# Two attention stages of one kernel: the order of scores, transposes, values and outputs on TensorE, and the last unit's end

## What is computed

```
# third block, the attention in front of the experts (x: 16 x 64 x 256, 16 heads of 16)
h = layernorm(x)
q, k, v = (h@wq+bq)*16**-0.5, h@wk+bk, h@wv+bv     # by head
p = softmax(q @ k.T)                                # 64 x 64 for each batch and head
x = x + (p @ v) @ wo + bo                           # then the experts

# fifth block, latent attention with a rotary part, causal
Q = concat(Qc, rope(Qr)); K = concat(Kc, rope(Kr))  # 16 + 8 wide
scores = where(causal, clip(Q @ K.T, -80, 80), -inf)
x = x + (softmax(scores / sqrt(24)) @ V) @ W_O
```

## Time and profile before

| | |
|---|---|
| time, median of 3 runs | 900.33 us (899.58 to 900.87) |
| the profiled execution: its own time, its span | 903.07 us, 901.3 us |
| PE, PEld busy, instructions | 763.8 us (85%), 510.4 us (57%), 7000 each |
| DVE, ACT, POOL busy | 569.3 us (63%), 428.8 us (48%), 314.9 us (35%) |
| granted TensorE clock over the span | 0.922 |
| block stage, first scores to last add | 440.04 to 481.73 |
| latent stage, first scores to last add | 789.33 to 830.95 |

### The profile page before, as it was taken

The page is one execution under the profiler, slowest core; times in us unless marked ns, Lnnn a source line. Parts: engine busy times, 40 slices in busy tenths (PEclk is TensorE's granted clock), DMA queues, the critical chain, the costliest instruction groups (busy, mean ns, idle before and its releaser), DMA issues. The chain is left out here.

```text
span 901.3 us, 19146 instructions
## 1 busy us (share of the span) xinstructions
PE 763.8 (85%) x7000; PEld 510.4 (57%) x7000; DVE 569.3 (63%) x1295; ACT 428.8 (48%) x1281; POOL 314.9 (35%) x379
## 2 busy tenths in 40 slices
PE   5999999698799999967777299999388886777996
PEld 4788888445333333345456288888267774365334
DVE  3565555539699999976796533222578776455474
ACT  3656666462565664234365100000367883655572
POOL 2111120027577888721350440100554432233002
PEclk9899999897799999998897599999679997989899
DMA  8011530000020000000001046542456310000001
GB/s 260 18 43 53 191 108 1 2 1 1 24 71 0 1 1 1 0 1 1 1 2 48 24 132 195 181 135 76 140 164 218 105 42 1 1 3 3 0 1 49
DMA packets 44893, 51.79 MB, mean 57 GB/s; under 512 B 7072, under 2 KB 40832, under 8 KB 44544
## 3 DMA queue, kind: packets, MB, share of 16 engines
q1 hardware_dynamic: 40256, 43.48, 15.5%
q0 software_dynamic: 1536, 4.20, 1.6%
q10 hardware_dynamic: 3008, 2.88, 0.9%
HBM read 45.31 MB, written 5.24 MB: 56 GB/s over the span
## 5 line engine op out<-in xcount | busy, mean ns | idle before, releaser
L968 PE MATMUL r_u_ps<-r_t_in,l_same_head 128*128 128x512 f32 x124 | 69.5, 643 | 1.4 <-DVE r_t_in L892 0.2
L1362 ACT ACTIVATE a_prob<-a_s_ps,a_negmax 128x256 f32<-128x256 f32 x128 | 59.1, 485 | 19.5 <-DVE a_negmax L1418 19.5
L936 POOL TENSOR_TENSOR r_q_in<-r_state,rec_q 128x512 f32<-128x512 f32 x62 | 68.0, 1097 | 0.0
L1737 ACT ACTIVATE a_prob<-a_s_ps,a_negmax 128x256 f32<-128x256 f32 x128 | 58.6, 482 | 19.4 <-DVE a_negmax L1773 18.4
L2334 PE MATMUL m_h_ps<-m_rowsT,l_w 128*128 128x256 f32 x256 | 58.7, 390 | 0.0
L1424 DVE COPY a_probT<-a_w_ps 128x512 f32<-128x512 f32 x48 | 31.5, 688 | 38.9 <-PE a_w_ps L1283 38.9
L1773 DVE TENSOR_REDUCE a_negmax<-a_s_ps 128x2 f32<-128x512 f32 x64 | 41.2, 684 | 22.6 <-PE a_s_ps L1653 19.7
L2334 PEld LDWEIGHTS m_h_ps<-m_rowsT,l_w 128*128 128x128 f32 x256 | 50.3, 197 | 7.2
L2345 PE MATMUL m_y_ps<-l_w,m_hidden 128*128 128x256 f32 x240 | 53.9, 379 | 0.0
L2380 ACT ACTIVATE m_rowsT<-m_xt_ps,l_B_s,l_B_g 128x256 f32<-128x256 f32 x16 | 8.2, 560 | 93.3 <-PE m_xt_ps L2322 86.7
L2248 DVE TENSOR_SCALAR m_hidden<-m_h_ps,l_b 128x256 f32<-128x256 f32 x64 | 28.0, 480 | 37.9 <-PE m_h_ps L2334 37.9
(11 more groups left out here) (388 smaller groups left out, 1881.5 us busy)
## 6 DMA issues: line engine op xcount, KB each, us to landing
l_w<-in_B_w SPq DMA_DIRECT2D x16, 1024.0 KB, 5.8
a_ctxT<-in_ctxT SPq DMA_DIRECT2D x31, 256.0 KB, 2.8
a_ctx<-in_ctx SPq DMA_DIRECT2D x16, 256.0 KB, 2.8
expert_out<-m_y ACTq DMA_DIRECT2D x7, 256.0 KB, 5.7
all_X<-in_x SPq DMA_DIRECT2D x4, 256.0 KB, 5.2
l_b<-in_B_b SPq DMA_DIRECT2D x1, 1024.0 KB, 5.3
all_xnT<-own_rows SPq DMA_DIRECT2D x1, 1024.0 KB, 6.5
routed_rows<-ffn_xn SPq DMA_DIRECT2D x8, 128.0 KB, 1.8
```

What stands on the lines that cost most here:

```text
L936: ins = nc.gpsimd.tensor_tensor(q_in[i % 2][m][:, :, :, :], twice(state[i % 2][m]), steps("q", 2 * i - 1, 2, m), ALU.mult)
L968: nc.tensor.matmul(u_ps[m][:, :, :, :], same_head[:, :], t_in[m][:, :, :, :], start=False, stop=True).then_inc(u_mm[m], 1)
L1362: ins = nc.scalar.activation(prob[n % 2][:, r, m, :], s_ps[r][:, m, :], ACT.Exp, bias=negmax[n % 2][:, r, m:m + 1], accum_out=den[n % 2][: ...
L1737: ins = nc.scalar.activation(prob[n % 2][:, r, m, :], s_ps[r][:, m, :], ACT.Exp, bias=negmax[n % 2][:, r, m:m + 1], accum_out=den[n % 2][: ...
```

## The change

- TensorE: scores(0) and scores(1) come first; then, in unit u, scores(u+2) stands behind the transposes of u and ahead of output(u-1) and values(u). In the last unit output(2) stands ahead of the transposes instead of behind them.
- The last unit's end is cut in two halves, one for each row tile: values, take_heads, output and add each run by half. The second half's values go into `s_ps0` and its output into `s_ps1`, which are free by then.
- The last unit's fourth scaling runs on VectorE instead of GpSimd, behind add(1).
- Latent stage alone (`bounded`): ScalarE takes one take_transposed(u) and one exps(u+1) in turn, and VectorE runs each sum with its reciprocal behind it, instead of each sum one ahead.

```diff
-                    pe.wait_ge(p_ready, ONE + 4 * u + n + 1)
+                    pe.wait_ge(*((last_p, ONE + 1) if (u, n) == (NU - 1, 3) else (p_ready, ONE + 4 * u + n + 1)))
...
+                    if u == NU - 1:
+                        pe.wait_ge(shifted_ready, ONE + 4 * NU)
                     of = {where(q): q for q in range(16)}
                     for i in range(2):
+                        out = last_o[i] if u == NU - 1 else o_ps[:, i, :, :]
...
-                    mm.then_inc(pv_mm, 1)
+                        if i == 1 or u == NU - 1:
+                            mm.then_inc(pv_mm, 1)
...
                 scores(0)
+                scores(1)
                 for u in range(NU):
-                    if u + 1 < NU:
-                        scores(u + 1)
+                    if u == NU - 1:
+                        output(u - 1)
                     for n in range(4):
                         transposes(u, n)
-                    if u >= 1:
+                    if u + 2 < NU:
+                        scores(u + 2)
+                    if 1 <= u < NU - 1:
                         output(u - 1)
                     values(u)
-                output(NU - 1)
+                for i in range(2):
+                    last_output(i)
...
+                def last_output(i):
+                    pe.wait_ge(heads_ready, ONE + NU + i)
+                    pe.wait_ge(x_added, ONE + NU - 1)
+                    for k in range(KD):
+                        mm = nc.tensor.matmul(last_out[i], headsT[:, i, k, :], WoT[:, k, :], start=(k == 0), stop=(k == KD - 1))
+                    mm.then_inc(out_mm, 1)
...
                 for u in range(NU):
-                    for r in range(4):
+                    for r in range(3 if u == NU - 1 else 4):
                         pool.wait_ge(rden_ready, ONE + 4 * u + r + 1)
...
+                def take_last_heads(i):
+                    act.wait_ge(pv_mm, ONE + NU + i)
+                    act.wait_ge(out_mm, ONE + NU - 1)
+                    if bv is None:
+                        ins = nc.scalar.activation(headsT[:, i, :, :], last_o[i], ACT.Copy)
+                    else:
+                        for m in range(KD):
+                            ins = nc.scalar.activation(headsT[:, i, m, :], last_o[i][:, m, :], ACT.Identity, bias=bv[:, m:m + 1])
+                    ins.then_inc(heads_ready, 1)
...
                 for u in range(NU):
-                    for r in range(3):
+                    for r in range(4):
+                        if not bounded and r == 3 and u + 1 < NU:
+                            exps(u + 1, 0)
                         take_transposed(u, r)
-                    if u + 1 < NU:
-                        exps(u + 1, 0)
-                    take_transposed(u, 3)
-                    if u + 1 < NU:
+                        if bounded and u + 1 < NU:
+                            exps(u + 1, r)
+                    if not bounded and u + 1 < NU:
                         for r in range(1, 4):
                             exps(u + 1, r)
...
-                    sums(u, 0)
+                    if not bounded:
+                        sums(u, 0)
                     for r in range(4):
-                        if r + 1 < 4:
+                        if bounded:
+                            sums(u, r)
+                        elif r + 1 < 4:
                             sums(u, r + 1)
                         reciprocals(u, r)
                     if u >= 2:
                         add(u - 2)
+                dve.wait_ge(rden_ready, ONE + 4 * NU)
+                nc.vector.tensor_tensor(of_bank(NU - 1, 3), of_bank(NU - 1, 3), rden[(NU - 1) % 2][:, 3, :].unsqueeze(2).to_broadcast([P, 8, T]), ALU.mult).then_inc(last_p, 1)
                 add(NU - 2)
-                add(NU - 1)
+                for i in range(2):
+                    dve.wait_ge(out_mm, ONE + NU + i)
+                    if bo is not None:
+                        dve.wait_ge(bias_added, ONE + NT)
+                    nc.vector.tensor_tensor(X[:, NT - 2 + i, :], last_out[i], X[:, NT - 2 + i, :], ALU.add).then_inc(x_added, 1)
```

More of the change, by code:

```diff
@@ L1914, in batch_attention_stage @@
         out_ps = sc.ps("out_ps", [P, 2, D])
-        (s_mm, top_ready, shifted_ready, exp_done, den_ready, rden_ready, p_ready, pt_mm, pt_ready, pv_mm, heads_ready, out_mm, x_added, bias_added) = (sc.sem(n) for n in (
-            "s_mm", "top_ready", "shifted_ready", "exp_done", "den_ready", "rden_ready", "p_ready", "pt_mm", "pt_ready", "pv_mm", "heads_ready", "out_mm", "x_added", "bias_added"))
+        (s_mm, top_ready, shifted_ready, exp_done, den_ready, rden_ready, p_ready, pt_mm, pt_ready, pv_mm, heads_ready, out_mm, x_added, bias_added, last_p) = (sc.sem(n) for n in (
+            "s_mm", "top_ready", "shifted_ready", "exp_done", "den_ready", "rden_ready", "p_ready", "pt_mm", "pt_ready", "pv_mm", "heads_ready", "out_mm", "x_added", "bias_added", "last_p"))
+        last_o = [o_ps[:, 0, :, :], s_ps[0][:, :, :].rearrange("p h t -> p (h t)")[:, 0:KD * P].rearrange("p (m q) -> p m q", m=KD)]
+        last_out = [out_ps[:, 0, :], s_ps[1][:, :, :].rearrange("p h t -> p (h t)")[:, 0:D]]
         def of_bank(u, r):
@@ L1968, in values @@
                                     pair = 4 * m + r
-                                    mm = nc.tensor.matmul(o_ps[32 * r:32 * r + 32, i, m, j * T:(j + 1) * T], vblk[:, 4 * u + 2 * i + j, pair, :],
+                                    mm = nc.tensor.matmul(out[32 * r:32 * r + 32, m, j * T:(j + 1) * T], vblk[:, 4 * u + 2 * i + j, pair, :],
                                                           probT[u % 2][:, of[i, pair], j * T:(j + 1) * T], start=True, stop=True)
-                    mm.then_inc(pv_mm, 1)
+                        if i == 1 or u == NU - 1:
+                            mm.then_inc(pv_mm, 1)
                 def output(u):
@@ L2030, in _ @@
                 for u in range(NU):
-                    for r in range(3):
+                    for r in range(4):
+                        if not bounded and r == 3 and u + 1 < NU:
+                            exps(u + 1, 0)
                         take_transposed(u, r)
-                    if u + 1 < NU:
-                        exps(u + 1, 0)
-                    take_transposed(u, 3)
-                    if u + 1 < NU:
+                        if bounded and u + 1 < NU:
+                            exps(u + 1, r)
+                    if not bounded and u + 1 < NU:
                         for r in range(1, 4):
                             exps(u + 1, r)
-                    take_heads(u)
+                    if u + 1 < NU:
+                        take_heads(u)
+                for i in range(2):
+                    take_last_heads(i)
             @block.vector
```

## The result

The changed kernel is slower: 903.79 us (median of 20 runs, 899.61 to 906.23) against 901.07 (20 runs, 899.58 to 903.61). The ratio is 1.0021, 95% interval 1.0011 to 1.0031, so +1.9 us where 1.15 less was forecast; the forecast had the sign wrong, and the median is outside its range. (Its sum was laid on 900.33, the median of three runs; on the 901.07 of twenty it would have been 899.9, which changes nothing of this.) The profiled execution has a span of 903.0 us (901.3 before) and a mean clock of 0.919 (0.922).

The account below looks back on a forecast made before the run. VectorE bounds the block stage; in the latent stage no engine is full and the loop round the engines sets the pace. Block +0.3 and latent -1.45 give -1.15 on 900.33: 899.2 us, range 897.3 to 901.1.

Parts of the forecast that it names:

- a stall of 0.5 on the full engine: Block stage loop: scores(3) waits for shift(2), output(0) comes later, and VectorE waits 0.5 us for add(0).
- 1.15 lost: Block stage end: output(2) ahead of the last transposes makes values(3) start at 478.1 against 476.95, 1.15 us later.
- The halves: Block stage end cut in halves: 3.9 us from values(3)'s start to the end against 4.78, a gain of 0.88.
- The sum of +0.3: Block stage in total: 1.15 us lost before values(3) less 0.88 gained by the halves, +0.3.
- The sum was -1.45: Latent stage in total: values(3) starts 0.45 us earlier and the end by halves gains 1.0, -1.45.
- I expect the stop again: Latent stage: TensorE's stop for late instructions comes again within values(0)'s last instructions, 1.2 to 1.5 us.
- It is given back at once: Latent stage loop: scores(3) starts 3.4 us earlier, but output(0) and values(1) now follow it, leaving 0.55 at transposes(2).
- The end by halves: Latent stage end: 3.54 us from values(3)'s start to the last add's end against 4.54, a gain of 1.0.
- number 2: Rival: the latent stage's instruction stop does not come back; -2.6 us, 897.7 us; chance 0.27.
- number 3: Rival: clock falls in the block stage while TensorE idles 2.75 us before output(2); about +2.0, 902.4 us; chance 0.10.
- Number 4: Rival: halved end and early scores give more than counted, no give-back in the latent stage; -3; chance 0.03.
- signs of being wrong: Last transposes not held by output(2), block-stage clock below 1.0 behind 470, or another stage moved by a microsecond.

Follow-up runs that it names:

- e3: Changed kernel plus idle identity transposes in the block stage, 9 before scores(2) and scores(3) each, 16 before output(2): ratio 0.9987 to the kernel before, block stage 42.33 us.
- e1: Changed kernel with the latent stage put back to the order and end of before, block stage as changed: ratio 1.0018 to the kernel before.
- e4: Changed kernel with output(2) behind the last unit's transposes again in both stages: ratio 0.9990 to the kernel before.
- e6: Changed kernel plus 100 small unused matmuls at the start of the stage ahead of the latent stage: ratio 1.0040 to the kernel before.
- e7: Changed kernel plus 28 idle identity transposes at the end of the stage ahead of the latent one: ratio 0.9989 to the kernel before.
- e10: Changed kernel plus 9 idle transposes before scores(2) and scores(3) each in the block stage, none before output(2): ratio 1.0005 to the kernel before.
- e2: Changed kernel with the block stage put back to the order and end of before, latent stage as changed: ratio 1.0005 to the kernel before.
- e11: Changed kernel plus 16 idle transposes before output(2) of the block stage alone: ratio 1.0025 to the kernel before.
- e5: Changed kernel with both stages back in the old order, keeping only the end in halves with its scaling on VectorE: ratio 0.9975 to the kernel before.
- e8: Changed kernel with old block order, halved end and idle transposes; latent output(2) behind the last transposes, 28 idle transposes ahead: 897.08 us, ratio 0.9925 to before.
- e9: As e8 without the idle transposes in the block stage: 900.06 us, ratio 0.9937 to the kernel before.
- e12: As e8 but with the latent stage in the order of before, keeping its halved end and the 28 idle transposes ahead: ratio 0.9957 to the kernel before.

## Why the forecast was wrong, step by step

**Block stage, the loop.** "S(3) now stands ahead of O(0) and V(1) and waits for it ... a stall of 0.5 on the full engine": right in itself, 0.48 in e3. The step that failed is the one behind it, that O(0) then takes 1.89. It took 3.46 at half clock, and the two falls together cost 3.3 us, which the sum had at nothing. I had looked for a fall behind 470 alone and priced it at +2.0 net, with a chance of 0.10; a wait of 1.41 us on TensorE was counted only by what it held back, not as idle time for the clock.

**Block stage, the end.** "1.15 lost" until V(3): 1.25 in e3. The halves: 0.92 gained against 0.88, from V(3)'s start 3.86 to the last add's end against 4.78. O(2) ahead of T(3) did as forecast. The sum of +0.3 is what e3 shows (+0.32); to it came 3.3 us of clock. The falls stood in all five profiles with this order of scores and no transposes added in the stage (changed, e1, e4, e6, e7), near the same places, and in none of the three with some added. The Trainium skill ("TensorE: Matmul & The Clock Gate", section "HAM oscillation — how this bites in real kernels") describes this loss, a burst, a wait, and the next burst slow; the trace agrees at 464 and 477, behind waits of 1.41 and 2.52 us. In e10 the same wait of 2.52 us cost nothing, so the wait alone doesn't decide it, and what does stays open.

**Latent stage.** The sum was -1.45, and +0.94 came, 2.39 more. Parted by the table and the timeline:

- The start, 0.60. T(0) began 9.99 us behind the stage's start against 9.39, since the clock was at half all through S(1). With the stage alike in code up to there and no transposes ahead of it, it came at 8.37 to 9.99 in six more runs with this order (e2, e3, e4, e6, e10, e11), and at 9.99 and 8.75 in two with the old (e1, e5). So this part is chance, and not the change's.
- The second stop, 1.61: the step that failed in this stage. "I expect the stop again, within V(0)'s last instructions, of 1.2 to 1.5": it came there, with 1.04, and S(2) and V(0) took 4.38 from 803.70 to T(1) at 808.08, against 4.4 costed. That there would be only one was wrong. I counted on from S(0) to the first border and not to the next, 256 instructions on, which falls into the long burst of S(3): S(3) took 3.64 (811.08 to 814.72), with a stop of 1.23 in it, where 2.03 was costed. A stop costs 0.3 to 0.4 beyond its listed idle time here.
- The other steps of the loop, 0.18 up to V(2), and -0.07 from V(2) to V(3): 6.83 against 6.9 costed and 7.26 before. So the 0.43 won there is a little more than costed; it was lost again ahead of V(2). "It is given back at once" was right.
- The end by halves, 0.07: 3.61 against the forecast's 3.54, and 4.54 before.

0.60 + 1.61 + 0.18 - 0.07 + 0.07 = 2.39.

The forecast costed O(2)'s place rightly, but didn't ask what the other place would give. In all seven runs with O(2) in front V(3) starts 6.83 or 6.84 behind V(2); in the three with it behind the last transposes (e4, e8, e9) it is 5.24. In front, TensorE waits 0.72 for take_heads(2), and nothing is left to fill the 0.69 that V(3) waits for the last take_transposed; behind, both are covered. From T(0) to V(3) less the stops the changed kernel took 26.72 us and the six others with O(2) in front 26.34 to 26.81, no better than the old order's 26.48 to 27.03 (before, e1, e5, e12); with O(2) behind it is 25.21 (e4), 24.39 (e8) and 24.83 (e9).

**The rest.** The scaling on VectorE took 0.74 and was hidden, as costed. The rivals: number 2 (no stop) is refuted; number 3 (clock) is what happened, once where it said, under O(2), and once earlier. That its 902.4 is nearer to the 903.79 than the forecast is in part luck, since it had neither the first fall nor the second stop. Number 4 (no give-back in the latent stage) didn't come. Of the signs of being wrong two showed: a clock below 1.0 behind 470, and other stages that moved. The stretch between the two stages, alike in code, is 302.74 us long against 307.28 before, and 304.0 to 307.5 in the other runs but e6; no run says why. How often the clock falls in an execution that isn't profiled stays open: the stage lengths would give +4.5 us, the timed runs +1.9 by the ratio (the profiled span +1.7), and the 20 times of the changed kernel spread over 6.6 us where those of before spread over 4.0.

## What to carry to other kernels

When a reordering makes TensorE wait in a new place, price the wait twice: by what it holds back, and by the work behind it at half clock if the clock falls; a few idle transposes in all the gaps tell which of the two it is (in one gap at a time they told nothing here). A change that is the sum of an order and a shorter end should be timed in its parts: here the ends alone were 0.25% faster, and the order took that away and more. Where a step moves ahead of another on an engine, its own length is spent in either place; the price is the wait that it now meets, and the wait that it no longer fills: 1.6 us for O(2) in the latent stage.

## What the runs showed of the hardware

- Instruction stops go by the count of TensorE's instructions, not by the work: in the latent stage each matmul with its load added ahead moves the stop back by one matmul, and it repeats every 256 instructions. Packets come at 799.0, 805.4 and 811.4 us in the changed kernel; the quick matmuls behind the second and the third come to a stop and resume 2.4 to 2.7 us after the packet; the first, under the half clock and with transposes behind it, stops nothing. In the latent stages here the stops over 0.5 us come to 0.8 to 2.8 us, and 400 instructions added far ahead turned 2.27 into 0.77. The Trainium skill ("Runtime: NRT & Kernel Launch", section "Instruction fetch mechanics") gives blocks of 256 instructions, which suits this period and the 57 packets for 14,000 instructions, and calls crossing from one to the next mostly hidden; for short matmuls issued in a row that isn't so here.
- Work that computes nothing can shorten a stage: 34 transposes in its gaps, 45.60 to 42.33 us, and the timed ratio from 1.0021 to 0.9987.
- Stages alike in code repeat to 0.01 us as long as the clock does the same: V(3) of the block stage stands at 41.46, 41.46, 41.46 and 41.47 in four kernels, and at 36.83 or 36.84 in four others, two of which only add idle transposes.
